# First edge stage of a four-layer graph network kernel: feature products in 64-row tiles, 30 batches summed by one-hot products

## The reference

```python
# L0, on edges e = (src -> dst) and reversed (dst -> src)
mi = concat([x[src_bi], x[tgt_bi], ef_bi], 1)                     # 128 + 128 + 64
h = relu(_layernorm(mi @ msg_w1 + msg_b1, ln1_g, ln1_b)) @ msg_w2 + msg_b2
agg = segment_sum(h, tgt_bi, num_segments=N)
upd = relu(_layernorm(concat([x, agg], 1) @ upd_w1 + upd_b1, ln2_g, ln2_b)) @ upd_w2 + upd_b2
# L1
p = exp(e - segment_max(e, src)[src]); p = p / segment_sum(p, src)[src]
```

## Time and profile before

| | us |
|---|---|
| median of 3 runs | 5516.4 |
| lowest, highest | 5498.99, 5519.98 |
| profiled execution | 5502.47 |
| its span, first to last instruction | 5500.7 |
| first edge stage in it | 49.6 to 2471.6 |

### The profile page before, as it was taken

The page is one execution under the profiler, slowest core; times in us unless marked ns, Lnnn a source line. Parts: engine busy times, 40 slices in busy tenths (PEclk is TensorE's granted clock), DMA queues, the critical chain, the costliest instruction groups (busy, mean ns, idle before and its releaser), DMA issues.

```text
span 5500.7 us, 93752 instructions
## 1 busy us (share of the span) xinstructions
PE 4667.1 (85%) x27053; PEld 3382.8 (61%) x27130; DVE 4598.5 (84%) x13377; ACT 3625.0 (66%) x12258; POOL 4078.2 (74%) x3715
## 2 busy tenths in 40 slices
PE   4899999999999999976888888488888886999995
PEld 3787777777777777755555555355555554545553
DVE  5899999999999999976888888588888876777776
ACT  4777777777777777752777776267677763555552
POOL 4788888888888888874777776577777755777776
PEclk7889999998999999987999899699999998999997
DMA  8867666666666666653677676466666652555553
GB/s 234 160 159 175 158 160 154 158 163 152 154 160 157 163 149 160 160 90 97 201 200 200 196 202 187 130 209 211 211 208 211 213 163 84 162 155 158 159 160 105
DMA packets 614740, 919.53 MB, mean 167 GB/s; under 512 B 104056, under 2 KB 324338, under 8 KB 613954
## 3 DMA queue, kind: packets, MB, share of 16 engines
q1 hardware_dynamic: 394530, 565.04, 32.5%
q0 software_dynamic: 219680, 348.31, 29.6%
HBM read 616.90 MB, written 299.48 MB: 167 GB/s over the span
## 4 chain that ended last, share of the span: by engine, by line
POOL 45%; issue 20%; PE 14%; DVE 13%; DMA 5%; ACT 2%; SPq 1%; POOLq 0%; DVEq 0%; ACTq 0%
POOL arena L1726 26%; POOL tab L1370 9%; POOL arena L1388 9%; PE PS L1889 2%; DMA arena<-T,srcI 2%; PE PS L2230 2%; DMA tab<-arena 2%; POOL arena L1421 2%; PE PS L1684 1%; PE PS L2208 1%; DVE arena L1173 1%; DVE arena L1138 1%; PE PS L986 1%; PE PS L988 1%; DVE arena L1146 1%
## 5 line engine op out<-in xcount | busy, mean ns | idle before, releaser
L1726 POOL DMA_INDIRECT arena<-T,srcI x2112 | 2020.8, 957 | 779.8 <-issue 631.5
L1370 POOL DMA_INDIRECT tab<-arena x680 | 1122.1, 1650 | 222.0 <-issue 205.5
L1388 POOL DMA_INDIRECT arena<-T,srcI x784 | 797.7, 1017 | 287.2 <-issue 282.0
L1713 DVE TENSOR_TENSOR_SCAN arena<-arena,PS 128x512 f32<-128x512 bf16 x588 | 748.3, 1273 | 162.2 <-PE PS L2535 82.8
L1693 ACT ACTIVATE arena<-PS 128x512 f32<-128x512 f32 x588 | 348.2, 592 | 635.8 <-PE PS L1684 635.8
L1793 DVE TENSOR_SCALAR arena<-PS,nodeid 128x512 bf16<-128x512 f32 x908 | 627.2, 738 | 75.7 <-PE PS L1774 75.7
L2517 PE MATMUL PS<-arena 128*128 128x512 bf16 x2323 | 550.7, 384 | 4.4 <-issue 0.4
L986 PE MATMUL PS<-We,arena 65*128 65x256 f32 x1568 | 490.6, 395 | 70.4 <-DVE arena L1046 50.2
L1889 PE MATMUL PS<-arena 128*128 128x396 bf16 x2800 | 542.6, 351 | 8.7 <-DVE arena L1793 7.3
L789 PE MATMUL PS<-arena 128*128 128x448 bf16 x2184 | 527.3, 400 | 0.8 <-DVE arena L802 0.8
L988 PE MATMUL PS<-arena 128*128 128x256 f32 x1568 | 481.4, 388 | 0.0
(11 more groups left out here) (319 smaller groups left out, 10945.0 us busy)
## 6 DMA issues: line engine op xcount, KB each, us to landing
H<-arena SPq DMA_DIRECT2D x784, 256.0 KB, 2.3
arena<-keepR SPq DMA_DIRECT2D x294, 256.0 KB, 4.7
arena<-wF SPq DMA_DIRECT2D x98, 512.0 KB, 5.2
arena<-T,srcI POOLq DMA_INDIRECT x2896, 3.6
arena<-in_ea64T SPq DMA_DIRECT2D x98, 256.0 KB
arena<-sH SPq DMA_DIRECT2D x98, 256.0 KB, 4.7
arena<-dH SPq DMA_DIRECT2D x98, 256.0 KB, 5.0
arena<-S SPq DMA_DIRECT2D x98, 256.0 KB
```

Source lines behind the costliest of these rows:

```text
L1370: e.indirect_dma_start(out=tabs[k % KT], out_offset=at_rows(iA[b % 10][:, c:c + 1]), in_=X2[n % 3][:, c, :], in_offset=None, compute_op=AL ...
L1388: e.indirect_dma_start(out=Gs[b % NR][:, c, :], out_offset=None, in_=T0, in_offset=at_rows(srcI[:, CB * b + c:CB * b + c + 1])).then_inc(g ...
L1713: ins = e.tensor_tensor_scan(s[b % n][:, h, :], kR[g % 6][:, h0:h0 + CB * P], src[h], s[(b - 1) % n][:, h, CB * P - 1:CB * P] if b else in ...
L1726: e.indirect_dma_start(out=dst[:, c, :], out_offset=None, in_=T_tab, in_offset=at_rows(srcI[:, CB * b + c:CB * b + c + 1])).then_inc(gs.of ...
```

## The change

- `edge_lists`: the bias msg_b1 is loaded by itself, centred, and added to the source half of every block of T0 by a one-row product (`onesF[0:1, :]` by `b1[0:1, :]`) behind each of the 25 products. We holds the 64 feature rows twice, on partitions 0-63 and 64-127, and no bias.
- `edge_rows`: the features of chunks 0 and 1 of a batch go to partitions 0-63, those of chunks 2 and 3 to 64-127, by two DMAs a group; eT is half as wide, and its row of ones is gone.
- `pe_C`: for k = 0, 1 the feature products of chunks k (upper 64 rows, bank 0) and 2 + k (lower 64 rows, bank 1) stand next to each other, then the two one-hot products of these chunks.
- `Spread(6, 30)` takes the place of `Spread(7, 26)`. The 14 steps of a pair now lie in 12 turns: `when` puts steps 0 and 1 in turn 0, steps 7 and 8 in turn 6, one in each other. The one-hot of a step is still built one turn earlier, a flush still comes one turn after its step.

```diff
@@ edge_lists
+                e.dma_start(b1[0:1, :], A["L0_gnn_msg_b1"].rearrange("(a n) -> a n", a=1)).then_inc(bias1, 16)
                 e.dma_start(sampI, row(A["dstC"][0, :], NCH)).then_inc(ld_first.of(0), 16)
...
-                e.dma_start(We[0:64, 0:P], w1[2 * P:2 * P + 64, :]).then_inc(ld_m.of(0), 16)
-                e.dma_start(We[64:65, 0:P], A["L0_gnn_msg_b1"].rearrange("(a n) -> a n", a=1)).then_inc(ld_m.of(0), 16)
+                for q in range(2):
+                    e.dma_start(We[64 * q:64 * q + 64, 0:P], w1[2 * P:2 * P + 64, :]).then_inc(ld_m.of(0), 16)
...
-                        ins = e.matmul(bank(g % 7)[:, k * 2 * P:(k + 1) * 2 * P], xT[:, b + k, :], W1ab[:, :],
-                                       start=True, stop=True)
+                        e.matmul(bank(g % 7)[:, k * 2 * P:(k + 1) * 2 * P], xT[:, b + k, :], W1ab[:, :],
+                                 start=True, stop=False)
+                        ins = e.matmul(bank(g % 7)[:, k * 2 * P:k * 2 * P + P], onesF[0:1, :], b1[0:1, :],
+                                       start=False, stop=True)
...
                 e.wait_ge(ld_w.of(0), ld_w.at(1))
+                e.wait_ge(bias1, 16)
+                center(e, b1[0:1, :], P, 1, 3)
...
@@ edge_rows
+            def at(src, q):
+                return src[:, c0:c0 + GE].rearrange("f (b q c) -> q f b c", b=2, q=2)[q]
...
             with e.Else():
-                e.dma_start(t, src[:, c0:c0 + GE]).then_inc(sem, 16)
+                for q in range(2):
+                    e.dma_start(t[64 * q:64 * q + 64, :, :], at(A["ea64T"], q)).then_inc(sem, 16)
@@ Spread
+                self.when = [u * 2 * M // 14 for u in range(14)]
...
-            def at(self, i):
-                s, u = divmod(i - self.first, 2 * self.M)
-                return (s, u) if 0 <= s < self.n // 2 and u < 14 else (None, None)
+            def turns(self, i):
+                s, v = divmod(i - self.first, 2 * self.M)
+                return [(s, u) for u in range(14) if self.when[u] == v] if 0 <= s < self.n // 2 else []
...
@@ L0_edges
-            pk = Spread(7, 26)
+            pk = Spread(6, 30)
...
-            eT = [arena.get(GE) for _ in range(2)]
+            eT = [arena.get(2, 2 * P) for _ in range(2)]
...
-                for c in range(CB):
-                    e.matmul(psC[:, c * 2 * P:(c + 1) * 2 * P], eT[g % 2][0:65, h0 + c * P:h0 + (c + 1) * P],
-                             We[0:65, :], start=True, stop=False)
-                    ins = e.matmul(psC[:, c * 2 * P:(c + 1) * 2 * P], OT[b % 2][:, c * P:(c + 1) * P], Tw[g % 2],
-                                   start=False, stop=True)
+                for k in range(2):
+                    for q in range(2):
+                        c, rows = 2 * q + k, slice(64 * q, 64 * q + 64)
+                        e.matmul(psC[:, c * 2 * P:(c + 1) * 2 * P], eT[g % 2][rows, b % 2, k * P:(k + 1) * P],
+                                 We[rows, :], start=True, stop=False)
+                    for c in (k, 2 + k):
+                        ins = e.matmul(psC[:, c * 2 * P:(c + 1) * 2 * P], OT[b % 2][:, c * P:(c + 1) * P], Tw[g % 2],
+                                       start=False, stop=True)
...
-                for t in eT:
-                    e.memset(t[64:65, :], 1.0)
```

More of the change, by code:

```diff
@@ L319, in edge_lists @@
             w1 = A["L0_gnn_msg_w1"]
+            b1, bias1 = v_[:, 0, :], one("s_bias1")
             dI = arena.get(NCH, dt=I32)
@@ L593, in dve @@
                 e.tensor_copy(flag[:, 1:2], PS[:, 3584:3585]).then_inc(s_dve, 1)
-                center(e, We[0:65, 0:P], P, 65, 2)
-                e.tensor_copy(We[0:65, P:2 * P], We[0:65, 0:P])
+                center(e, We[:, 0:P], P, P, 2)
+                e.tensor_copy(We[:, P:2 * P], We[:, 0:P])
                 with is_unsorted(e, "dve"):
@@ L685, in edge_lists, with edge_rows @@
             return Stage(sp, pe, dve, act, pool)
-        def edge_rows(e, n0, n, t, c0, sem):
-            src = A["ea64T"] if n == 64 else A["ea32T"]
+        def edge_rows(e, t, c0, sem):
+            def at(src, q):
+                return src[:, c0:c0 + GE].rearrange("f (b q c) -> q f b c", b=2, q=2)[q]
             with e.If(unsorted["sp"] > 0):
-                e.dma_start(t, eTs[n0:n0 + n, c0:c0 + GE]).then_inc(sem, 16)
+                for q in range(2):
+                    e.dma_start(t[64 * q:64 * q + 64, :, :], at(eTs[0:64, :], q)).then_inc(sem, 16)
             with e.Else():
-                e.dma_start(t, src[:, c0:c0 + GE]).then_inc(sem, 16)
+                for q in range(2):
+                    e.dma_start(t[64 * q:64 * q + 64, :, :], at(A["ea64T"], q)).then_inc(sem, 16)
         class Spread:
@@ L760, in dve_onehot, with onehot @@
             def dve_onehot(self, e, i):
[L762 to L765, removed]
+                for s, u in self.turns(i + 1):
+                    if u % 4 < 2:
+                        self.onehot(e, s, u // 4, u % 4)
+            def onehot(self, e, s, q, h):
                 if 4 * s + q >= 1:
@@ L776, in pe_step, with step_of @@
             def pe_step(self, e, i):
[L778 to L781, removed]
+                for s, u in self.turns(i):
+                    self.step_of(e, s, u // 2, u % 2)
+            def step_of(self, e, s, j, h):
+                u = 2 * j + h
                 e.wait_ge(self.oh.of(0), self.oh.at(8 * s + j // 2 * 2 + h))
@@ L794, in dve_flush, with flush @@
             def dve_flush(self, e, i, accT):
[L796 to L799, removed]
+                for s, u in self.turns(i - 1):
+                    if u % 2:
+                        self.flush(e, s, u // 2, accT)
+            def flush(self, e, s, j, accT):
                 e.wait_ge(self.step.of(0), self.step.at(14 * s + 2 * j + 1))
@@ L847, in L0_edges @@
             gx = take("gx", NBAT, 1, 16 * CB)
-            ld_e, ld_s, ld_w, ld_d = [take(n, NG, 2, 16) for n in ("le", "ls", "lw", "ld")]
+            ld_e = take("le", NG, 2, 32)
+            ld_s, ld_w, ld_d = [take(n, NG, 2, 16) for n in ("ls", "lw", "ld")]
             ld_k, ld_t = [take(n, NG, 2, c) for n, c in (("lk", 16), ("lt", 32))]
@@ L869, in sp_rows @@
                     e.wait_ge(C.of(0), C.at(2 * g - 3))
[L870 removed]
+                edge_rows(e, eT[g % 2], g * GE, ld_e.of(g))
                 if g >= 2:
@@ L977, in pe_C @@
             def pe_C(e, b):
-                g, h0 = b // 2, b % 2 * CB * P
+                g = b // 2
                 if b % 2 == 0:
```

## The result

The changed kernel takes 5771.6 us (median of 4 runs, 5756.1 to 5779.2), the kernel before 5513.9 us beside it: ratio 1.0477, interval 1.0461 to 1.0492. The forecast was 5524 us, no change, with 5588 as the upper end: 248 us too low.

The account below looks back on a forecast made before the run. GpSimd was taken to bound the first edge stage, VectorE and TensorE close below. -31.3 + 36 + 9.5 = +14 us on 5502.5 gives 5517; laid between two bases (profiled run, earlier median 5516.4), 5524 us, range 5483 to 5588.

Parts of the forecast that it names:

- GpSimd's pace: First edge stage: 16 fewer scatters at 1.96 us take 31.3 us off GpSimd's bound, if nothing else takes over.
- The period of six: First edge stage: six batches take 72.2 us, with GpSimd at 71.0, VectorE 70.9 and TensorE 70.3.
- The +36: First edge stage: loss from engines waiting for each other, 30 x (72.2 - 71.0) us.
- The tiles: Edge feature products: half overlap saves 0.43 us a batch, two tile round trips cost 0.68; net +0.25 on TensorE.
- The order of the new turns: First edge stage: 14 steps in 12 turns add waits between VectorE and TensorE, 0 to 1.5 us a period.
- the ninth step: Edge stage: TensorE's ninth step waits for a flush VectorE issues a turn later; counted within 0 to 1.5 us a period.
- The bias in the table: List stage: 16 one-row products at 0.56 us before line 568, plus 0.5 for the bias DMA: +9.5 us.
- My bound for the low clock: List stage: with the clock at the low level throughout, the bias products cost +13 us instead of +9.5.
- What costs nothing: Two feature DMAs instead of one, centring the doubled We and two one-row memsets: no added time.
- set the pace: Rival: GpSimd still bounds the edge stage, -31.3 + 9.5 = -22 us, 5495 to 5502; chance 0.2.
- TensorE as the bound by tiles or switches: Rival, edge stage: tiles don't overlap or switches cost more; +65 us, 5580; chance 0.25.
- The builds' late waits: Rival: VectorE's one-hot builds wait late each period, 2 us more; +38 to +50 us, 5560; chance 0.1.

Follow-up runs that it names:

- the order was mended: Changed kernel with VectorE's flush moved behind dve_S2 and steps 6 and 7 sharing turn 5 instead of 7 and 8 in turn 6: 5542.7 us, 1.0052.
- at full height with zeros: Changed kernel with old spreading (every seventh batch, 26) and the bias product at full height, bias in row 0 of a zeroed tile: 5509.5 us, 1.0003.
- all mended: Changed kernel with later flush, steps 6 and 7 in one turn, full-height bias product, count product four groups earlier: 5522.9 us, 1.0020; again 5523.4, 1.0023.
- ND = 4: Later flush, steps 6 and 7 together, full-height bias, early count, plus one scaling per batch moved from VectorE to ScalarE: 5507.7 us, 0.9993 to kernel before.

## Why the prediction was wrong, point by point

- **GpSimd's pace (-31.3 us): the mechanism right, the price not.** It issues 664 scatters for 680. But 1.96 and 1.32 us were taken as fixed, while part of them was the surplus beside the builds, which the change makes more of. That gives the gain back: 16.3 us more from the first scatter to the last, once the order was mended.
- **The period of six, 72.2 us: right once the order was mended** (144.2/2 = 72.1), with GpSimd at about 72.1 and not at 71.0 with VectorE in the way. The +36 that I took from it was too small even so. It counted from 84.1 us for seven batches, which is 144.2 for twelve; that stretch is a slow one, and the mean from 500 to 2200 us is 143.3. Between the scatters the kernel with the order mended is 16.3 us longer, not +36 - 31.3 = +5; 0.9 us a period over 15 periods is 14 of it. In the change itself the period of six is 80.2.
- **The tiles (+0.25 us a batch): wrong in sign.** The trace of after, single passes:

```profile
1046.85 0.70 PE L1003 MATMUL PS<-We,arena 64*128 64x256 f32 x4 [0.89 <-DVE arena L1064]
1047.48 1.13 PE L1006 MATMUL PS<-arena 128*128 128x256 f32 x4
1048.54 0.70 PE L1003 MATMUL PS<-We,arena 64*128 64x256 f32 x4
```

  A pair's four passes are over in 0.63 us where two products took 0.87. The single starts are 1046.850, 1046.857, 1047.141 and 1047.177: the first passes of both halves together, then the second ones. I had argued from program order that only one pass could overlap, and took a saving of 0.43 us for one of 0.87. The switch costs 0.2 us ahead of the full-height products (1.06 from 1047.48 to 1048.54 for 0.87) and 0.2 ahead of the pair: 0.39 us a round trip, near the 0.34 of the earlier trace rows. A batch takes 3.29 us from 1046.85 to the node sums at 1050.14, and 0.1 ahead of it for the switch, where eight products of the earlier trace rows take 3.48: -0.1 us.
- **The order of the new turns (0 to 1.5 us a period): this step failed**, and it made 218 of the 253.6 us (the edge stage of after, 2665.3 us, less that of the kernel with the order mended, 2447.1). I listed the waits that the change adds, three builds and the wait of the ninth step. I did not list the waits that it only moves: the flush waits on TensorE in every second turn of both kernels. It had cost 0.3 us in 2000, because its steps closed in light turns. I wrote down that odd turns are TensorE's heavy ones and used it for the doubled turns alone. Of the ninth step I priced the flush, not the turn that VectorE needs to come to it.
- **The bias in the table (+9.5 us): right in place, mis-sized; it is 20.** The one-row product costs 0.72 us for 0.56, and the 16 old table products, which I had left at 0.62, cost 1.15. My bound for the low clock (+13) doubled the added work only. Two terms were missed: the low level on all passes (0.62 us a block), and a round trip of 0.59 us at this level for the 0.34 of the earlier trace rows. A change that keeps TensorE slow is paid on all passes of the stretch.
- **What costs nothing: held.** No wait for the features' two DMAs stands among those of the edge stage. The one wait for a load ahead of a feature product, 20.7 us at the stage's start, is put down to the rows of the target table.
- **The rivals.** GpSimd did not set the pace in the change; it set it again once the order was mended, but at the higher prices. TensorE as the bound by tiles or switches did not occur. The builds' late waits were the nearest, at 2 us a period of six for some 8. The test that I gave, a period above 73.5 us, is met, and the list stage's start of VectorE moved by 20 us, not 9.5.

## What to carry to other kernels

Where loops are ordered by hand, check for each wait in a changed schedule, old ones too, in which turn its producer ends, and how late in that turn: a wait of 0.3 us in the trace may be cheap by parity alone. Give two dependent steps in one turn only if nothing of another engine stands between them. And take an engine's price per instruction as a mean over its neighbours: before multiplying it, see which instructions of the other engines stretch it, whether the change makes more of those, and whether it stands them in longer rows.

## What was not expected of the hardware

- Products of 64 rows on the two halves of the array overlap in full with 32-bit operands: both first passes start 7 ns apart, both second ones 2 to 36 ns, mostly 7. Going to a full-height product and back costs 0.39 us.
- One-row products among full-height ones keep all passes at the durations of the 1.2 GHz level, for over 30 us in the list stage. The windows view's 1.00 is no measurement there: the trace has no entry of the clock before 83.3 us; at full height with zeros the passes are short from about 14 us of the timeline on. Going to one row and back cost 0.59 us at the durations of the low level, and 0.34 in the earlier trace rows.
- GpSimd's indirect DMA instructions last 1.61 and 1.00 us, and beside comparisons from 16-bit to 16-bit on VectorE 2.08 and 1.67 us on average with all mended, up to 4.66 with ND = 4. Eight comparisons in a row cost them 2.0 us of surplus, four 0.4 to 0.5.
